# Aggregation by units of 128 places, experts chosen for two blocks at once, one-hots of the low digits made on ScalarE

## The reference

```python
h = (tokens @ W_gat).reshape(M, 4, 4)
e = leaky_relu(a_src[src] + a_dst[dst], 0.2)
alpha = exp(e - segment_max(e, dst)[dst]) / segment_sum(...)[dst]
agg = segment_sum(h[src] * alpha[:, :, None], dst)
scores = layernorm(agg).reshape(M, 4, 4).mean(1)
topk_s, topk_i = top_k(scores, 2)            # two of four experts
out = sum over e of gate[e] * (gelu(t @ W1[e] + b1[e]) @ W2[e] + b2[e])
```

## Time and profile before

| | |
|---|---|
| median of 3 runs | 4157.47 us |
| profiled execution | 4160.54 us, span 4158.8 us |
| busy: TensorE, VectorE, ScalarE, GpSimd | 67%, 78%, 27%, 67% of the span |
| mean granted TensorE clock | 0.803 of 2.4 GHz |
| second stage | from about 1320 us to the end |

### The profile page before, as it was taken

The page is one execution under the profiler, slowest core; times in us unless marked ns, Lnnn a source line. Parts: engine busy times, 40 slices in busy tenths (PEclk is TensorE's granted clock), DMA queues, the critical chain, the costliest instruction groups (busy, mean ns, idle before and its releaser), DMA issues.

```text
span 4158.8 us, 58181 instructions
## 1 busy us (share of the span) xinstructions
PE 2783.3 (67%) x19194; PEld 2162.5 (52%) x19194; DVE 3235.2 (78%) x5615; ACT 1122.5 (27%) x997; POOL 2780.4 (67%) x2785
## 2 busy tenths in 40 slices
PE   4488433358885277777777777777777776677775
PEld 1255322246563266665655556565565555556553
DVE  8877999988885477777778777787777777777775
ACT  0011000001111233343334333433333333333332
POOL 3000388888875777777777777777777777777771
PEclk8799655568887578888888887888888888888887
DMA  1133211169998921222222222222222222222283
GB/s 54 32 94 94 64 45 45 45 70 122 116 115 119 119 48 41 56 55 51 56 51 56 51 51 51 53 54 41 57 54 51 56 51 51 49 53 45 50 51 17
DMA packets 383237, 253.16 MB, mean 61 GB/s; under 512 B 302146, under 2 KB 337538, under 8 KB 382596
## 3 DMA queue, kind: packets, MB, share of 16 engines
q1 hardware_dynamic: 295284, 220.70, 25.6%
q0 software_dynamic: 87552, 29.20, 9.5%
q10 hardware_dynamic: 144, 0.00, 0.0%
HBM read 179.40 MB, written 70.24 MB: 60 GB/s over the span
## 4 chain that ended last, share of the span: by engine, by line
POOL 31%; issue 15%; DVE 11%; PE 7%; SPq 2%; DVEq 1%; DMA 1%; ACT 0%; ACTq 0%
POOL gath L1219 31%; PE C L1333 2%; DVE acc L1508 2%; PE C L1317 2%; PE A L1356 1%; PE A L1364 1%; SPq L1139 1%; DVE A L1573 1%; DVE nodes L1574 1%; DVE C L1473 1%; DVE picked L1469 1%; PE A L1346 1%; DVEq L1111 1%; DMA tab_d<-nodes 1%; SPq L1186 1%
## 5 line engine op out<-in xcount | busy, mean ns | idle before, releaser
L1219 POOL DMA_INDIRECT gath<-tab_d,src_no x2116 | 1998.3, 944 | 645.9 <-issue 644.0
L1333 PE MATMUL C<-spread,lo_hot 128*128 128x160 f32 x4360 | 844.7, 359 | 711.8 <-DVEq L1510 557.4
L1333 PEld LDWEIGHTS C<-spread,lo_hot 128*128 128x128 f32 x4360 | 769.3, 234 | 845.3 <-DVEq L1510 671.8
L486 POOL DMA_INDIRECT edge_d<-run_slots,slots x544 | 675.7, 1242 | 600.3 <-ACT run_slots L685 437.8
L1317 PEld LDWEIGHTS C<-damp,lo_hot_t 128*128 128x128 f32 x4384 | 547.1, 202 | 115.1 <-issue 115.1
L1317 PE MATMUL C<-damp,lo_hot_t 128*128 x4384 | 555.6, 283 | 53.6 <-ACT lo_hot_t L1238 36.5
L1508 DVE TENSOR_TENSOR acc<-acc,C 128x160 f32 x1090 | 347.8, 319 | 267.3 <-DVE C L1473 100.3
L598 PE MATMUL C<-wide_rec,hot_lo 128*128 128x136 f16 x2048 | 271.8, 304 | 300.3 <-DVE wide_rec L886 300.3
L598 PEld LDWEIGHTS C<-wide_rec,hot_lo 128*128 128x128 f16 x2048 | 241.8, 123 | 351.5 <-DVE wide_rec L886 294.2
L1495 DVE TENSOR_TENSOR spread<-hi_hot,C 128x2560 f32<-128x2560 f32 x137 | 386.4, 2820 | 4.7
L1271 ACT ACTIVATE nodes<-A,b2s 128x512 f32<-128x512 f32 x196 | 134.7, 687 | 862.4 <-PE A L1356 862.4
(11 more groups left out here) (282 smaller groups left out, 3292.1 us busy)
## 6 DMA issues: line engine op xcount, KB each, us to landing
lo_rows<-lo_d SPq DMA_DIRECT2D x137, 512.0 KB
gath<-tab_d,src_no POOLq DMA_INDIRECT x2116
pixels<-in_x SPq DMA_DIRECT2D x32, 392.0 KB, 7.9
src<-in_x SPq DMA_DIRECT2D x32, 392.0 KB, 9.3
nodes<-t_d SPq DMA_DIRECT2D x98, 128.0 KB
nodes<-x_d SPq DMA_DIRECT2D x98, 128.0 KB, 3.0
out<-nodes SPq DMA_DIRECT2D x784, 16.0 KB
edge_d<-run_slots,slots POOLq DMA_INDIRECT x544
```

The lines of the kernel that those rows point to most:

```text
L486: pool.indirect_dma_start(edge_d, bass.IndirectOffsetOnAxis(ap=slots[:, k, c:c + 1], axis=0), run_slots[:, k, c * RUN:(c + 1) * RUN, :].re ...
L1219: pool.indirect_dma_start(gath[:, g % BUFS, j, :], None, node_d if g < BUFS else tab_d, bass.IndirectOffsetOnAxis(ap=src_no[:, t:t + 1], a ...
L1333: mm = pe.matmul(C[:, bank, at:at + HI * VALS], lo_hot[:, g % UNROLL, u * U + j, :], spread[:, u * U + j].rearrange("p h v -> p (h v)"), s ...
```

## The change

- U goes from 2 to 1 and UG from 8 to 16: at most 2,132 units of 128 places in 134 groups of 16 tiles (2,132 tiles where there were 2,180). A unit is still one addition of 128 x 160 on VectorE, and a pair of units now has two tiles.
- `lo_hot` moves to ScalarE: for each tile an Abs of `lane` minus the digit (16 instructions of 128 x 128, `slot_gaps`, in two halves), then one Relu over 128 x 2048 (`slot_match`). They stand between the expert steps' instructions. `lo_less`, the negated digits, is made once.
- `choose` takes two blocks at once, 23 times, and the last three blocks singly: 26 in place of 49. The first three instructions and the last one stay one per block; the others are twice as wide. The steps of a pair of blocks are spread over the groups to the next choice: 64 groups have two steps (25 follow a choice and hold none, 3 hold one), 64 have one, 6 none.
- `raw` is loaded in four copies of 32 partitions (before two of 64), and `field` splits in four parts. Tiles are laid over one another to save memory; GpSimd's fill of `edge_d` at the start takes 16 DMAs of half the size.

```diff
-U = 2
-UNIT_RUN_BITS = 6
+U = 1
+UNIT_RUN_BITS = 5
-UG = 8
+UG = 16
...
-FULL_AFTER = [-(-((j + 1) * MAX_UNITS // NB) // UG) for j in range(NB)]
+CHOICES = [(j, j + 1) for j in range(0, NB - 3, 2)] + [(j,) for j in range(NB - 3, NB)]
+FULL_AFTER = [-(-((js[-1] + 1) * MAX_UNITS // NB) // UG) for js in CHOICES]
+STEP_AT, ends = [], 0
+for c, js in enumerate(CHOICES):
+    steps = len(js) * EXPERTS
+    begins = max(FULL_AFTER[c], ends)
+    ends = max(FULL_AFTER[c + 1], begins + steps // 2) if c + 1 < len(CHOICES) else NG
+    STEP_AT += [begins + n * (ends - begins) // steps for n in range(steps)]
...
+                    if g >= 2:
+                        act.wait_ge(s["lo_hot_ready"], g)
                     act.activation(lo_gap[:], lo_rows[:, g % LO_BUFS, :], ACT.Abs, bias=lane_no[:], scale=-1.0).then_inc(s["lo_gap_ready"], 1)
...
+                def slot_gaps(g, half):
+                    if half == 0:
+                        act.wait_ge(s["lo_hot_t_ready"], max(g + 1, 2))
+                        if g:
+                            act.wait_ge(s["lo_hot_ready"], g)
+                    for t in range(half * G // 2, (half + 1) * G // 2):
+                        act.activation(lane_gap[:, t, :], lane[:], ACT.Abs, bias=lo_less[:, g * G + t:g * G + t + 1]).then_inc(s["lane_gaps"], 1)
+                def slot_match(g):
+                    k = g % UNROLL
+                    act.wait_ge(s["lane_gaps"], (g + 1) * G)
+                    if g >= UNROLL:
+                        act.wait_ge(s["scattered"], (g - UNROLL + 1) * PAIRS)
+                    act.activation(lo_hot[:, k].rearrange("p t e -> p (t e)"), lo_gap[:], ACT.Relu,
+                                   bias=ones[:, 0:1], scale=-1.0).then_inc(s["lo_hot_ready"], 1)
...
                 for g in range(NG):
                     if g + 2 < NG:
                         lane_match(g + 2)
-                    for j, e in steps_due(g):
+                        slot_gaps(g + 2, 0)
+                    for j, e in steps_due(g)[0:1]:
+                        gelu(j, e)
+                    if g + 2 < NG:
+                        slot_gaps(g + 2, 1)
+                    for j, e in steps_due(g)[0:1]:
+                        expert_out(j, e)
+                    if g + 2 < NG:
+                        slot_match(g + 2)
+                    for j, e in steps_due(g)[1:2]:
                         gelu(j, e)
                         expert_out(j, e)
...
                     if pairs[0] == 0:
                         pe.wait_ge(s["spread_ready"], g + 1)
+                        pe.wait_ge(s["lo_hot_ready"], g + 1)
...
+                dve.tensor_scalar(lo_less[:], row_i, -1.0, None, ALU.mult).then_inc(s["lo_less_ready"], 1)
...
-                    dve.tensor_tensor(lo_hot[:, k], lane_v.rearrange("p (k h) -> p k h", k=1).broadcast_to([P, G, P]),
-                                      lo[:, g * G:(g + 1) * G].rearrange("p (t k) -> p t k", k=1).broadcast_to([P, G, P]),
-                                      ALU.is_equal).then_inc(s["lo_hot_ready"], 1)
...
+                    for k, j in enumerate(CHOICES[c]):
+                        rows = slice(k * HI, (k + 1) * HI)
+                        here = acc[:, bass.ds(block_at(dve, j), HI), :]
+                        L(dve.tensor_scalar(stat[:, rows], here[:, :, FEAT:VALS], 1e-16, None, ALU.add))
+                        L(dve.reciprocal(stat[:, rows], stat[:, rows]))
```

More of the change, by code:

```diff
@@ L1048, in build @@
             nodes = tb("nodes", [P, NQ, ROW])
-            lo = tb("lo", [P, LO_CHUNKS * P], BF16)
             hi = tb("hi", [P, TILES], BF16)
@@ L1069, in build @@
             T, hid, plain, X1 = late[:, 0:2], late[:, 2:4], late[:, 4:6], late[:, 6:6 + X_BUFS]
[L1070 to L1080, removed]
+            gate = tb("gate", [P, 4, HI, EXPERTS])
+            na_row = na[:].rearrange("p q f -> p (q f)")
+            mine_2, square_2 = (na_row[:, k * 2 * HI * FEAT:(k + 1) * 2 * HI * FEAT].rearrange("p (q f) -> p q f", f=FEAT) for k in range(2))
+            half_2 = na_row[:, 4 * HI * FEAT:5 * HI * FEAT].rearrange("p (q f) -> p q f", f=FEAT // 2)
+            beats_2 = na_row[:, 5 * HI * FEAT:5 * HI * FEAT + 4 * HI * EXPERTS * EXPERTS].rearrange("p (k q e f) -> p k q e f", k=2, q=2 * HI, e=EXPERTS)
+            stat_2 = tb("stat", [P, 2 * HI, EXPERTS])
+            logit_2 = tb("logit", [P, 2 * HI, EXPERTS])
+            odds_2 = tb("odds", [P, 2 * HI, EXPERTS])
+            one_2 = tb("one", [P, 2 * HI, 2])
+            root_2 = tb("root", [P, 2 * HI, 2])
+            rank_2 = tb("rank", [P, 2 * HI, EXPERTS])
             beta = tb("beta", [P, EXPERTS])
@@ L1121, in gates_due @@
             def gates_due(g):
-                return [j for j in range(NB) if FULL_AFTER[j] == g + 1]
+                return [c for c in range(len(CHOICES)) if FULL_AFTER[c] == g + 1]
             def steps_due(g):
                 return [(j, e) for j in range(NB) for e in range(EXPERTS) if STEP_AT[j * EXPERTS + e] == g]
-            raw = lo_hot[:].rearrange("p b t l -> p (b t l)").bitcast(F16)[:, 0:PLACES * RUN * FIELDS]
-            RAW_WORDS = PLACES * RUN * FIELDS // 2
+            raw = hots[:].bitcast(F16)[:, 0:PLACES * RUN * FIELDS]
             @block.sync
@@ L1271, in expert_out, with odds_of @@
                     act.activation(plain[:, v % 2], A[:, 2, :], ACT.Identity, bias=b2s[:, e:e + 1]).then_inc(s["expert_out"], 1)
-                def odds_of(j):
-                    act.wait_ge(s["exp_in"], j + 1)
-                    act.activation(odds[:], logit[:], ACT.Exp).then_inc(s["exp_ready"], 1)
+                def odds_of(c):
+                    n = len(CHOICES[c]) * HI
+                    act.wait_ge(s["exp_in"], c + 1)
+                    act.activation(odds_2[:, 0:n], logit_2[:, 0:n], ACT.Exp).then_inc(s["exp_ready"], 1)
                 lane_match(1)
+                act.wait_ge(s["lo_less_ready"], 1)
                 for g in range(2):
                     raw_factors(g)
+                    for half in range(2):
+                        slot_gaps(g, half)
+                    slot_match(g)
                 for g in range(NG):
@@ L1288, in _ @@
                         raw_factors(g + 2)
-                    for j in gates_due(g):
-                        odds_of(j)
+                    for c in gates_due(g):
+                        odds_of(c)
                 for j, e in steps_due(NG):
@@ L1528, in choose @@
                     L(dve.tensor_scalar(one[:, :, 0], one[:, :, 0], 1.0 / FEAT, None, ALU.mult))
-                    L(dve.tensor_tensor(mine[:], mine[:], wide(one[:, :, 0:1], FEAT), ALU.subtract))
-                    L(dve.tensor_tensor(square[:], mine[:], mine[:], ALU.mult))
-                    L(dve.tensor_tensor(mine[:], mine[:], over(vecs[:, 1, :], FEAT), ALU.mult))
-                    L(dve.tensor_reduce(one[:, :, 1], square[:], AX.X, ALU.add))
+                    L(dve.tensor_tensor(mine, mine, wide(one[:, :, 0:1], FEAT), ALU.subtract))
@@ L1533, in choose @@
+                    L(dve.tensor_tensor(square, mine, mine, ALU.mult))
+                    L(dve.tensor_tensor(mine, mine, over(vecs[:, 1, :], FEAT), ALU.mult))
+                    L(dve.tensor_reduce(one[:, :, 1], square, AX.X, ALU.add))
                     L(dve.tensor_scalar(one[:, :, 1], one[:, :, 1], 1.0 / FEAT, 1e-5, ALU.mult, ALU.add))
```

95 lines of the change are left out of this document (51 added, 44 removed).

## The result

The changed kernel takes **4536.08 us** (median of 4 runs, 4522.16 to 4542.77) where the kernel before took 4161.98 beside it (4 runs): a ratio of **1.089 [1.0865, 1.0915]**. The forecast was 4250: the sign was right, but the loss was four times as large. The profiled execution took 4522.16 us with a span of 4520.4.

What follows compares the result with a forecast made beforehand. GpSimd's gathers seemed the bound, VectorE nearly as slow and last after the change. VectorE's terms, TensorE and the start summed to +93 us on 4160.5, less 3 for the median: 4250 us, 2.2% slower, range 4110 to 4365.

Steps and rivals of the forecast that it cites:

- (h): TensorE's refill of the banks, without the cover of `lo_hot` between the halves of the additions: +25 us, bounds 0 and +100.
- (a): VectorE no longer makes `lo_hot`, 137 instructions of 2.29 us, each with a gap of 0.03: -319 us.
- (b): VectorE's additions stay at 319 ns, 1.03 us from pair to pair, 1,066 pairs in place of 545: +537 us.
- (c): Register loads ahead of a group's first addition on VectorE, 1.11 us for 16 in place of 0.79 for 8: +40 us.
- (d): Three groups fewer on VectorE, each 5.2 us without the terms priced elsewhere: -16 us.
- (e): Choices on VectorE: a pair of blocks takes 14.0 us in place of 20.6, 23 pairs: -151 us.
- (f): VectorE, now the last engine, no longer waits for gathered rows: -40 us.
- (g): VectorE's waits in late steps, 61 of 2.4 us, 146 in place of 141: +5 us, bounds -31 to +115.
- ScalarE: One-hots of the low digits, 7.0 us a group, Abs at about 0.31 us, fit in ScalarE's idle time: cost nothing.
- Start: Start of the second stage, with four copies of the sorted edges and eight casts: +12 us, bounds +5 and +20.
- TensorE at the low level: Rival: TensorE at 1.2 GHz in every group's additions, each losing up to 2.4 us: 4545 us, chance 0.07.
- GpSimd keeps the pace: Rival: VectorE's group falls under 19.97 us and the gathers set the end: 4110 us, faster, chance 0.18.

Runs made afterwards that it cites:

- lo_dve: The changed kernel with the one-hots of the low digits back on VectorE, between the halves of the additions: 4614.67 us.
- up_copy: The changed kernel with the matmuls of `up` run once more, without effect on the result, in TensorE's pause ahead of the third pair: 4504.12 us.
- up_early: The changed kernel with `up` of a group's first step moved from behind the fourth pair of the scatter to behind the second: 4362.01 us.
- fused_place: `fused` with `up` of the first step back between the fourth and the fifth pair: 4262.14 us.
- hold: `up_early` with the matmuls of `up` run twice more in the same pause, without effect on the result: 4334.62 us.
- fused: `early_regs` with a pair's second addition raising `pair_added` itself, in place of a separate increment: 4140.35 us, 0.995 of the kernel before.
- early_regs: `up_early` with a group's 16 registers loaded behind the issue of `spread_out`, in the group before: 4208.5 us.

## Why the prediction was wrong

The sign was right and so was the bound: VectorE became the last, GpSimd waits for it (296.2 us), and no wait for rows is left. The size was not. **The step that failed is (h), "TensorE": +25, with bounds 0 and +100, where the runs show about +250.** The prediction had worked out the loss of one group ("such a group loses up to 2.4 us": the low level, `up` between the halves). Then it took a quarter of that for the 25 groups behind a choice and 10 us for all others, because one group after a choice had lost nothing; and among the rivals it held the stretch's mean clock of 0.84 against the low level in every group. Both were read in a kernel where `lo_hot` still stood between the halves. The pause that it looked for behind choices is in nearly every group after: the step, the pick, sixteen registers and the first pair take VectorE's time while TensorE, with both banks full, stands idle: 3.11 us in the group shown, 3.89 in that of `lo_dve`. Three things must meet for the loss, and taking away any one takes most of it: the low level behind the pause (`up_copy`'s 19 groups), `up` behind the fourth pair (`up_early`, `fused_place`), and no cover there (`lo_dve`). What is left without `up` in that place is for more than half the low level too (`hold`).

The terms in turn, against the profiled span (forecast 4251.8, measured 4520.4: 268.6 more):

- (a) **`lo_hot`**: forecast 2.33 us per group with its gap; `up_early`'s timeline shows 0.15 us from the end of `hi_hot` to the next addition, which `lo_hot` had covered, and in the kernel before it was 2.25 us, 2546.39 to 2548.64. So it gave 2.10, 0.23 less: +31 over 134 groups. The rows are those of the kernel before:

```profile
2546.10 0.29 DVE L1429 TENSOR_TENSOR hi_hot<-C,hi 128x128 f32<-128x128 f32 x1
...
2548.64 0.77 DVE L1508 TENSOR_TENSOR acc<-acc,C 128x160 f32 x2
```

- (b) **Additions**: 321 ns, and 1.03 to 1.04 us between pairs that don't wait. Right.
- (c) **Registers**: 169.4 us ahead of the first addition in 130 groups, from the fifth to the end, 1.30 each in place of 1.11: +25. The line through two rows was too flat.
- (d), (e) **Groups and choices**: a pair's choice 14.0, as forecast.
- (f) **Gather wait**: gone, as forecast; from the fifth group to the end it had been 47.6 us and not the 39.8 of the window: -8.
- (g) **Late steps**: 148.0 us for 61, forecast 146 for 61: +2.
- (h) **TensorE**: 249 us, of which 3 lie ahead of a group's first addition and stand under (c); 246 in place of 25, +221.
- **ScalarE**: 59.9% busy from 2500 to 3000 (forecast about 70% at a faster cycle); its small Abs run at 0.305 us one behind another, as forecast, and no wait for `lo_hot` shows. Right.
- **Start**: forecast +12. The fifth group's `picked` came at 1493.99 us, 2 earlier than before (1496.06): -14. GpSimd's later start didn't count as long as VectorE was the last. The **tail** from the last `picked` to the end was 68.8 us in place of 61.3: +8.

31 + 25 - 8 + 2 + 221 - 14 + 8 = 265 of the 268.6. Each term is read to a few us, so that close a sum is luck in part; that (h) is by far the largest is not.

Of the rivals, "TensorE at the low level" gave 4545 and came within 9 us of the result, with a chance of 0.07. It named the right engine, the right pairs and the right level, and the prediction's own list of signs against itself had them ("gaps between pairs that grow to TensorE's"). That its number came so near is luck in part: it put 322 us (134 * 2.4) on the additions where some 250 are shown. And it is not the clock alone: with the mean clock as low (0.83), `up_early` has less than a third of the excess. The Trainium skill ("TensorE: Matmul & The Clock Gate", A second HAM failure mode: psum-queue depth-cycling) says that short idle times between groups of matmuls, as banks are cycled, make the clock swing between its levels. The trace agrees as far as it goes: 0.81 us for four records at the high level, about 1.2 behind a pause of 3.11 us. It doesn't show that pauses of 0.2 to 0.3 us between pairs do it: behind those the four took 0.81.

"GpSimd keeps the pace" (4110) needed "additions at 0.92 a pair"; `fused` has 0.93 and early registers besides, and reached 4140. Its sum had 12 us for the start, which took 26.7, and nothing for the tail, which took 15: together the 30 us between the two.

## What to carry to other kernels

An instruction that is taken off the last engine may be the cover of another engine's delay: before it is priced at its duration, follow what the other engine does in that time, and in what order its queue holds it, with the cover gone. A mean clock over a stretch doesn't tell where in a group the low level lies; read it in the rows behind each group's longest pause. When an edit fails to bring about what it was meant to, look in its trace for the groups in which it did. And where two engines share the end, a saving on one is worth nothing until the other's work falls too: the two small edits that gave 222 us in one kernel gave none in the other.

## What the runs showed of the hardware

- Sixteen register loads took 1.29 us on VectorE's queue where eight took 0.79, and next to nothing when they were issued behind an instruction of 2.82 us (`early_regs`: 140.1 us of `issue` became 4.3).
- A separate increment behind a pair's second addition cost 0.1 us: 0.25 idle in place of 0.15 between pairs.
- In the group shown, behind an idle time of 3.11 us, TensorE's granted clock was 0.50 (1.2 GHz) in the next eight records and in `up`, and 1.00 in the last pairs. One extra product of four records in that idle time left `up` at 1.13 us in only 19 of 126 groups (`up_copy`); three in all raised the mean from 0.83 to 0.91 (`hold`).
